# A macaron transformer layer on eight cores: more tiles of x loaded up front, a re-timed prologue, filler matmuls and feed-forward halves issued one ahead

## The reference, cut to what matters

```python
def layer(x):                                    # x: [8, 2048, 1024] f32
    x = x + 0.5 * ffn(layernorm(x))
    x = x + attention(layernorm(x))
    x = x + 0.5 * ffn(layernorm(x))

def ffn(xf):                                     # a routed feed-forward
    cluster = argmax(calibrate(xf @ cluster_sigs.T))          # 8 clusters
    tile = argmax(calibrate(xf @ sigs.T) inside that cluster)  # 8 tiles in each
    comp = tanh(gelu(xf @ compress_w1 + b1) @ compress_w2 + b2)
    mag = spline network of the chosen tile, on comp           # one number per token
    return layernorm(xf + mag * directions[tile] * output_scale) * gamma + beta

def attention(xf):                               # causal, 16 query heads, 4 key/value heads
    return layernorm(softmax(q @ k.T / 8, causal) @ v) @ Wo + bo
```

## Time and profile before

| what | us |
|---|---|
| median of 3 runs | 626.51 (624.59 to 629.09) |
| the profiled execution, its own time | 627.83 |
| its span, from the first to the last instruction, core 3 | 626.2 |
| spans of the eight cores | 618.3 to 626.2 |
| TensorE busy | 480.0 (77%) |
| ScalarE busy | 411.8 (66%) |
| VectorE busy | 383.7 (61%) |
| GpSimd busy | 99.6 (16%) |

### The profile page before, as it was taken

How to read it: one execution, slowest core, us unless ns; L and a number is a source line. 1 busy time by engine, 2 the same in 40 slices (tenths; PEclk the granted TensorE clock), 3 DMA queues, 4 the chain that set the end, 5 groups by cost and what they waited for, 6 DMA issues and landing times.

```text
span 626.2 us, 14665 instructions; the slowest of 8 cores (618.3 to 626.2 us)
## 1 busy us (share of the span) xinstructions
PE 480.0 (77%) x5156; PEld 276.7 (44%) x5156; DVE 383.7 (61%) x1134; ACT 411.8 (66%) x459; POOL 99.6 (16%) x187
## 2 busy tenths in 40 slices
PE   0426697782987799978998779889979998876832
PEld 0314353551454455644564334444545554443321
DVE  4756874787648565683443463657857774767444
ACT  1667745797428976796769764758877783995220
POOL 1212102342011221221112210100110110111000
PEclk9965887996999689996999898999999998798865
DMA  8969300224300310004008000030270152113101
GB/s 202 210 130 241 75 2 1 44 44 99 45 10 9 77 36 10 19 10 86 7 4 154 10 19 9 6 81 14 85 153 6 24 145 73 27 40 144 68 0 69
DMA packets 66652, 38.94 MB, mean 62 GB/s; under 512 B 59520, under 2 KB 61696, under 8 KB 66452
## 3 DMA queue, kind: packets, MB, share of 16 engines
q1 hardware_dynamic: 63204, 30.13, 19.9%
q0 software_dynamic: 2800, 5.77, 5.9%
q10 hardware_dynamic: 576, 2.10, 1.2%
HBM read 21.27 MB, written 8.39 MB: 47 GB/s over the span
## 4 chain that ended last, share of the span: by engine, by line
PE 49%; DVE 14%; ACT 11%; issue 9%; DMA 9%; POOL 3%; SPq 3%; DVEq 1%; ACTq 0%; POOLq 0%
PE pALL L95 49%; ACT sE L237 7%; DMA sX<-x 5%; DVE sX L205 3%; DVE sST L229 3%; DMA sT<-sXN 2%; SPq L101 2%; ACT sXN L237 2%; POOL sE L1037 2%; ACT L237 1%; POOL sRS L201 1%; ACT sHT L237 1%; PE pTR L193 1%; DVEq L123 1%; DVE sU L201 1%
## 5 line engine op out<-in xcount | busy, mean ns | idle before, releaser
L237 ACT ACTIVATE sE<-pALL,sNB 128x1024 bf16<-128x1024 f32 (+1 forms) x288 | 289.1, 1069 | 98.0 <-PE pALL L95 87.1
L95 PE MATMUL pALL<-sVTM,sE 128*128 128x65 bf16 x2176 | 111.5, 199 | 20.0 <-POOL sE L1037 18.0
L95 PE MATMUL pALL<-sQT,sKT 64*128 64x256 bf16 (+1 forms) x1152 | 105.4, 281 | 22.5 <-ACT sE L237 19.8
L95 PEld LDWEIGHTS pALL<-sVTM,sE 128*128 128x128 bf16 x2176 | 89.9, 100 | 68.7 <-issue 56.9
L1037 POOL TENSOR_SCALAR_AFFINE_SELECT sE<-sE 128x256 bf16<-128x256 bf16 x128 | 56.0, 439 | 309.5 <-ACT sE L237 300.3
L205 DVE SCALAR_TENSOR_TENSOR sX<-pALL,sRS,sX 128x512 f32<-128x512 f32 x96 | 70.8, 745 | 27.5 <-PE pALL L95 26.5
L95 PE MATMUL pALL<-sWQ,sT 128*128 128x512 bf16 x256 | 66.3, 392 | 6.6 <-issue 4.1
L95 PE MATMUL pALL<-sT,sWQ 128*128 128x512 bf16 x256 | 61.1, 389 | 0.8 <-DVE sQT L197 0.8
L95 PEld LDWEIGHTS pALL<-sQT,sKT 64*128 64x128 bf16 x1152 | 40.6, 96 | 47.2 <-issue 34.8
L237 ACT ACTIVATE sXN<-sX,sNM,sRS 128x1024 bf16<-128x1024 f32 x30 | 36.9, 1239 | 22.8 <-DVE sNM L205 14.0
L229 DVE BATCH_NORM_STATS2 sST<-sX 128x6 f32<-128x512 f32 x68 | 44.3, 675 | 4.4 <-DMA sX<-x 4.4
(11 more groups left out here) (172 smaller groups left out, 565.1 us busy)
## 6 DMA issues: line engine op xcount, KB each, us to landing
y<-sX SPq DMA_DIRECT2D x16, 512.0 KB, 2.9
sX<-x SPq DMA_DIRECT2D x12, 512.0 KB, 12.0
sX<-x ACTq DMA_DIRECT2D x4, 512.0 KB, 9.4
sWQ<-wq POOLq DMA_DIRECT2D x2, 1024.0 KB, 23.8
sWQ<-wo POOLq DMA_DIRECT2D x1, 2048.0 KB, 15.1
sT<-sAN SPq DMA_TRANSPOSE x39, 2.4
sSG<-sd SPq DMA_DIRECT2D x1, 512.0 KB, 12.1
sW1C<-cw POOLq DMA_DIRECT2D x1, 512.0 KB, 11.3
```

Of the source, the lines that this page charges most:

```text
L95: return self.op("t", lambda e: e.matmul(out, lhsT, rhs, start=start, stop=stop, **kw), *after, ns=self.array(n))
L237: return lambda e: e.activation(*a, **k)
```

## The change

The change has these parts:

- **Loads.** Tiles 0 to 7 of x are issued by ScalarE at the start. The keys' weights wait for tile 5 of x, the first half of the queries' weights for tile 7, the second half for the first, tiles 12 to 15 of x for the values' weights. The assumed arrival times change.
- **Ring.** `xn_ring` has seven slots in the prologue. The four new ones are the buffers sE of attention, which are unused until then.
- **Planner.** `COST["v"]` is 500 ns in the prologue: a VectorE step that is ready earlier than another may be passed only if it would end more than that ahead. ScalarE's clock starts at 5 us.
- **Table fetches.** The exp of sE72 for batch 1 is issued after the tanh of that batch and replaces a dummy exp there.
- **Filler matmuls.** Where the planner sees TensorE idle for over 100 ns in the prologue and its use low, `hum` adds a matmul of sIDB with itself, 256 columns wide, into a free PSUM bank, where nothing reads it. There are 112 of them.
- **Tails.** `ffn_tail` issues the matmuls of one half ahead before the VectorE instruction of the half before, in the prologue and after the last attention block.

```diff
+    def low(self):
+        return self.use < 0.45 * (self.clock["t"] + 300.0 - self.stretch)
...
-COST = {"t": 0.0, "v": 0.0, "s": 0.0, "g": 0.0, "y": 0.0}
+COST = {"t": 0.0, "v": 500.0, "s": 0.0, "g": 0.0, "y": 0.0}
...
-                if tag in wanted and wanted[tag] < start + COST[tag]:
+                if tag in wanted and wanted[tag] < start + (COST[tag] if groups[0] == 0 else 0.0):
...
+        if groups[0] == 0 and now > 32e3 and soonest - now > 100.0 and P.low() and hum():
+            continue
...
-    for t, at in enumerate((6.5e3, 9.7e3, 13.5e3, 18e3)):
+    for t, at in enumerate((6.7e3, 9.7e3, 13.5e3, 18e3, 22e3, 24.5e3, 27e3, 29.5e3)):
         load_x("s", t, at)
...
-        yield "g", xt[2]
-        W["k"] = load("g", "Lwk", sWK, d_wk, 29.5e3, xt[3])
-        for t in range(4, 8):
-            load_x("y", t, 23.5e3 + 2.3e3 * t, xt[3])
+        yield "g", xt[5]
+        W["k"] = load("g", "Lwk", sWK, d_wk, 35e3, xt[5])
+        for t in range(8, 12):
+            load_x("y", t, 37e3 + 4.5e3 * (t - 8), xt[7])
...
-    xn_ring = Banks(range(3))
+    xn_ring = Banks(range(7))
+    def xn(i):
+        return sXN[:, i] if i < 3 else sE[:, i - 3].rearrange("p h q -> p (h q)")
...
-        yield "s", z
-        st[k] = {"exp": op("s", I.activation(E72, E72, AF.Exp), z, ns=400)}
+        def exps():
+            st[k]["exp"] = op("s", I.activation(E72, E72, AF.Exp), z, ns=400)
+        st[k] = {}
+        if k != 1:
+            yield "s", z
+            exps()
...
         if k == 1:
-            op("s", I.activation(sRS3[:, 0:1], sHF[:, 8:9], AF.Exp), ns=200)
+            exps()
+            P.clock["s"] += 1300.0
...
+                due.append((t, half, i, bank, m))
+                while len(due) > (1 if count[0] == 0 or 3 in ATT else 0) or due and (j, half) == (n - 1, 1):
+                    yield from ffn_add(k, rs2, *due.pop(0))
...
+    def hum():
+        b = fring.best()
+        if b is None or fring.when(b) > P.clock["t"]:
+            return False
+        P.mm(pALL[:, b, 0:256].rearrange("p (a n) -> p a n", a=2), sIDB[:], bc(sIDB[:].rearrange("p (o n) -> p o n", o=1), 1, 2), True, True, tidb, fring.free[b], n=256)
+        return True
```

More of the change, by code:

```diff
@@ L495, in th_loads @@
     def th_loads():
-        yield "g", xt[2]
-        W["k"] = load("g", "Lwk", sWK, d_wk, 29.5e3, xt[3])
-        for t in range(4, 8):
-            load_x("y", t, 23.5e3 + 2.3e3 * t, xt[3])
-        yield "g", None
[L502 to L510, removed]
+        yield "g", xt[5]
+        W["k"] = load("g", "Lwk", sWK, d_wk, 35e3, xt[5])
+        for t in range(8, 12):
+            load_x("y", t, 37e3 + 4.5e3 * (t - 8), xt[7])
+        yield "g", xt[7]
+        W["q"] = [load("g", "Lwq0", sWQ[:, :, 0:512], d_wq[:, :, 0:512], 49e3, xt[7])]
+        yield "g", W["q"][0]
+        W["q"].append(load("g", "Lwq1", sWQ[:, :, 512:1024], d_wq[:, :, 512:1024], 65e3, W["q"][0]))
+        yield "g", None
+        W["v"] = load("g", "Lwv", sWV, d_wv, 70e3)
+        for t in range(12, NT):
+            load_x("y", t, 74e3 + 2.5e3 * (t - 12), W["v"])
+    P.clock.update(s=5e3, y=6e3, g=9e3)
     def cst(c, n=1):
@@ L866, in ffn_chain, with ffn_add @@
         CHAIN[k] = True
+    def ffn_add(k, rs2, t, half, i, bank, m):
+        hs = slice(512 * half, 512 * (half + 1))
+        yield "v", m
+        x = v(I.scalar_tensor_tensor(sX[:, t, hs], pALL[:, bank, :], sRS2[:, t:t + 1], sX[:, t, hs], ALU.mult, ALU.add, accum_out=sSU[:, t, half:half + 1] if k < 2 else None), m, rs2, ns=740)
+        fring.give(i, x)
+        if half:
+            done[t] = x
+            DONE[t] = True
+            if k >= 4:
+                yield "y", x
+                P.dma("y", "ST", dy[128 * t:128 * (t + 1), :], sX[:, t, :], x)
     def ffn_tail(k):
@@ L870, in ffn_tail @@
         wt, rs2 = st[k]["wt"], st[k]["rs2"]
+        due = []
         for j in range(n):
@@ L1254, in th_chain @@
     def th_chain(k):
-        while k not in st:
+        while k not in st or "exp" not in st[k]:
             yield None
@@ L1308, in build_program @@
     others = [Thread(g) for part in first for g in part]
-    weave(P, None, others, 0.0, lambda: (0, 0) in NBREADY, count)
+    def hum():
[4 more added lines that the diff above has]
+        return True
+    weave(P, None, others, 0.0, lambda: (0, 0) in NBREADY, count, hum)
     fring.slots = [6, 7]
-    weave(P, None, others, 0.0, lambda: fring.held <= {6, 7}, count)
+    xn_ring.slots = [0, 1, 2]
+    weave(P, None, others, 0.0, lambda: fring.held <= {6, 7} and xn_ring.held <= {0, 1, 2}, count, hum)
+    e_free[:] = [xn_ring.free[3 + j] for j in range(4)]
     for tag in ("t", "s"):
@@ L1315, in build_program @@
     for J, rate in enumerate((1400.0, 900.0, 800.0, 1200.0)):
-        weave(P, None, others, 0.0, lambda: (J, 0) in NBREADY, count)
-        weave(P, Thread(attn(J)), others, rate, None, count)
+        weave(P, None, others, 0.0, lambda: (J, 0) in NBREADY, count, hum)
+        weave(P, Thread(attn(J)), others, rate, None, count, hum)
     fring.free.update({0: s_free[0], 1: s_free[0], 2: s_free[1], 3: s_free[1], 4: o_free[0], 5: o_free[1]})
     fring.slots = [6, 7, 0, 1, 2, 3, 4, 5]
-    weave(P, None, others, 0.0, lambda: not any(th.live for th in others), count)
+    weave(P, None, others, 0.0, lambda: not any(th.live for th in others), count, hum)
     last = Tok("g")
```

42 lines of the change are left out of this document (17 added, 25 removed).

## The result

The changed kernel takes 634.29 us (633.41 to 637.11, 4 runs) where the one before takes 626.09 on the same chip: a ratio of 1.0141, 95% interval 1.0113 to 1.0169. It is slower, by 1.4%. The profiled execution took 637.11 us, the longest of the four, and its slowest core is core 2 with a span of 635.6 us. In all that follows, medians and ratios leave out executions in which one die ran at a lower clock than the other.

What follows compares the result with a forecast made beforehand. The prologue up to attention's first exp was taken as serial; its 4.4 us gain, with end and attention at 0, gave 626.5 - 4.5 = 622.0 us. The forecast's own range was 617 to 627, with attention's bounds 612 to 630.

Steps and rivals of the forecast that it cites:

- Loads (part 1): Prologue, batch 0: VectorE's 5.30 us stall for tile 4 goes; sOHP ends at 44.6 us, a gain of 2.3 us.
- Fillers (part 2): Prologue to sWT: fillers of 0.213 us each, 18 then 22, cost 1.1 us with tile 5's transposes; sWT at 55.1 us.
- what they may give back I count at nothing: Prologue: fillers' full clock for 0.6 us transposes and first tail halves counted as 0, those matmuls lying beside VectorE's evacuations.
- The rival with fillers ahead of the chain: Prologue: up to 51 fillers stand before sOHP, parameters and sWS, 10.9 us at low clock, giving 633 us; chance 0.08.
- Keys and first exp (parts 3 and 4): sWT to first attention exp: keys start at 71.3 us, 7.0 earlier; exp at 97.3 against 101.76, 4.4 us gained.
- The end (part 5): Projection and last tails after attention: small gains and costs counted as nothing, bounds -1.5 and +1 us.
- Attention: First exp onward: planner's picks differ with the same instructions; no sign from the profile, 0, bounds -4 and +5 us.
- Neither waits long: Attention, 101.7 to 580 us: TensorE busy 405 of 478 us, ScalarE 345, neither said to wait long.
- everything up to the last mark is serial: Prologue to first attention exp: time saved there comes off the span, if attention takes as long as before.
- The second rival: Nothing comes of the loads: tile 5 lands at 27.9 us or attention's other order returns the gain; 626 us, chance 0.20.

Runs made afterwards that it cites:

- square of runs: Old and new prologue, each with old and new order after it: 625.8 and 633.4 us with the old prologue, 628.9 and 634.3 with the new.
- x2: Prologue of the kernel before, with the changed kernel's order played back from the first attention step: 633.4 us, ratio 1.0116.
- n1: Kernel before with 300 ns added once to the planner's TensorE clock as attention comes, nothing physical changed: 630.5 us, ratio 1.0076.
- n8: Kernel before with new loads and seven slots alone, planner free, its TensorE clock 300 ns back as attention comes: 633.0 us, ratio 1.0177.

## Why the prediction was wrong

The forecast was 622.0 us, range 612 to 630; 634.29 lies above it.

*Loads (part 1).* The positions were right: tile 5's copy at 25.26 against 24.6, sOHP's end 44.57 against 44.6. The gain of 2.3 us was one of core 3: on the median core sOHP ends 0.5 us later than before, since the two copies and squares stand ahead of the exp on every core and the wait for tile 4 was long only on some (5.73 us of ScalarE on core 3, none on core 1). The two edits of this part alone gave 622.6 us, 0.9941.

*Fillers (part 2).* The sizes were off, without harm to the start: 18 fillers take 2.80 us from the first to the last, 0.156 each instead of 0.213, because part of them runs at full clock. TensorE then waits 1.14 us for sOHP, and 2.59 for sWS behind the 22, so neither group stands in the way. The place where I was wrong is "what they may give back I count at nothing": with them the start comes 3.5 us earlier and the rest takes 3.9 to 7.0 us more, about 4 of which are ScalarE work left for later. The rival with fillers ahead of the chain gave a time near the measured one (633) by a mechanism that didn't happen.

*Keys and first exp (parts 3 and 4).* Right within 1.2 us (first sKT) and 0.4 us (exp). But the sum took core 3's gain of 4.4 us, the slowest core of one execution, and took it for pure gain, while three normalizations and two evacuations had moved behind the first exp. On the median core it is 1.9 us: the first exp before was spread over 6.9 us between cores, and the change removed the spread more than it moved the middle. The slowest core of the end need not be the one that started last.

*The end (part 5).* Right: nothing clear of noise (633.4 without this part, 634.3 with it).

*Attention.* This is the step that failed: "0, bounds -4 and +5 us". The stretch took 532.1 instead of 523.5 us on the median core (+8.6), and 538.7 instead of 524.4 on the slowest (+14.3). I had treated the other order as noise around nothing. Two readings behind that were wrong. "Neither waits long" overlooked 133 us of 478 in which ScalarE is idle, and 98.0 us of idle time ahead of the exps, 87.1 of them on TensorE, in the costliest row of the page before: there was room for an order to be worse. And "everything up to the last mark is serial" left out that the planner can pass work over that mark. The second rival had the mechanism in half a sentence ("attention returns the gain by another order"), but priced it at the gain and no more, 626 us. The square of runs gives 5.4 to 7.6 us of the slowest-core time to that order. With the planner's clock moved by 300 ns either way, the stretch ranged from 516.0 to 527.2 us. The order before looks like a good draw: behind the same prologue another order was clearly slower in four cases (the changed kernel, x2, n1, n8) and clearly faster in none. A new one was then more likely worse than better, and my bounds were about centred on nothing. The range was also added up wrongly: 617 - 4 and 627 + 5 are 613 and 632, not 612 and 630; 634.29 lies above either.

*Not settled:* what else than the 2.1 us of moved ScalarE work makes the new prologue with the old order lose 3.8 us from the first exp on (527.3 against 523.5), all of which goes with the fillers (520.3 without them); and which few picks of the planner make one order slower than another.

## What to carry to other kernels

Where a planner with its own clock interleaves the work, every edit draws a new order of all that follows, and that can outweigh the edit. Hold the order (write it down and play it back) to measure the edit, then draw several orders and keep the best; here loads and slots gave 0.994 with the old order held and 0.993 with the best of three draws, while the whole change gave 1.014. An earlier start of a stage is a gain only if the same work has been done by then: count the instructions ahead of the mark, before and after. And a wait read on the slowest core may be one of that core alone; look at the others before it goes into a sum.

## What the runs showed of the hardware

Filler matmuls kept TensorE's granted clock at 0.81 where it had been 0.50 (38 to 56.4 us, core 2 after and core 3 before). In three pairs they gained nothing in all (628.9 and 625.6, 634.3 and 634.3, 626.5 and 622.6 us with and without), and in none of them did sWT, the end of the dependent chain that they run beside, come clearly earlier (53.6 and 53.7, 54.3 and 53.8, 55.2 and 53.6 us).

In attention, the granted clock had fallen to 0.50 before TensorE waited 3.19 us for a transpose, and stayed there. Ten key matmuls then took 4.43 us, where fifteen took 3.40 at full clock in the other order: the wait cost its own time, and the lower level some 2.2 us more (4.43 - 3.40 x 10 / 15).

A load that is issued behind small constants can land at very different times on the eight cores: the copy of tile 4 began between 30.2 and 36.8 us before. With the tiles first in their queue, the copy of tile 5 began between 24.2 and 25.3 us.
